# Router logits with the router's columns as loaded weights in the four column quarters of TensorE

## What is computed

```python
shared = geglu(xf, w1s, w2s, w3s)
logits = xf @ Wg                       # (2048 x 256) @ (256 x 8)
idx = jnp.argmax(logits, axis=-1)
for e in range(N_EXPERTS):
    y = geglu(xf, W1[e], W2[e], W3[e])
    final = final + jnp.where((idx == e)[:, None], y, 0.0)
```

## Time and profile before

| | us |
|---|---|
| median of 3 runs | 510.26 |
| lowest, highest | 509.38, 511.22 |
| the profiled execution, its own time | 505.81 |
| its span, first to last instruction | 504.2 |

### The profile page before, as it was taken

How to read it: one execution, slowest core, us unless ns; L and a number is a source line. 1 busy time by engine, 2 the same in 40 slices (tenths; PEclk the granted TensorE clock), 3 DMA queues, 4 the chain that set the end, 5 groups by cost and what they waited for, 6 DMA issues and landing times.

```text
span 504.2 us, 9444 instructions
## 1 busy us (share of the span) xinstructions
PE 492.4 (98%) x2928; PEld 433.9 (86%) x2929; DVE 320.6 (64%) x529; ACT 248.9 (49%) x378; POOL 75.1 (15%) x97
## 2 busy tenths in 40 slices
PE   8999999999999999999999899999999999999994
PEld 7799888888888889898888788988988988988884
DVE  2577768768767778667544876734775568375335
ACT  3676774565653563424444574534572556272220
POOL 4421031011011001004340100100100001000570
PEclk9999999999999999999999999999999999999999
DMA  4997010000000004001342545620745175300235
GB/s 128 359 319 229 2 42 1 0 1 2 1 1 1 1 0 168 2 0 49 129 168 94 207 174 195 237 75 21 239 151 192 41 271 176 127 27 15 73 96 177
DMA packets 20586, 52.81 MB, mean 105 GB/s; under 512 B 3280, under 2 KB 14544, under 8 KB 16592
## 3 DMA queue, kind: packets, MB, share of 16 engines
q0 software_dynamic: 5328, 28.32, 16.0%
q1 hardware_dynamic: 15232, 24.15, 14.0%
HBM read 41.71 MB, written 10.75 MB: 104 GB/s over the span
## 4 chain that ended last, share of the span: by engine, by line
PE 84%; issue 4%; DVE 4%; DMA 3%; POOL 2%; ACT 1%; POOLq 0%; DVEq 0%; SPq 0%
PE ps L246 26%; PE ps L248 25%; PE ps L247 25%; PE ps L686 3%; POOL fetched L429 2%; PE ps L589 1%; DMA first_stage<-tok_w_in 1%; PE ps L604 1%; PE ps L531 1%; DMA q<-codebook_in,idx_sb 1%; PE ps L566 1%; PE ps L578 1%; DVE stats L1021 1%; DMA fetched<-y_sorted,pos 1%; DVE fetched L1327 1%
## 5 line engine op out<-in xcount | busy, mean ns | idle before, releaser
L956 DVE TENSOR_TENSOR hT<-ps,hT 128x512 fp32r<-128x512 f32 x64 | 43.9, 686 | 38.7 <-ACT hT L761 21.4
L246 PE MATMUL ps<-w_slots,xTp 128*128 (+1 forms) x160 | 64.2, 401 | 1.6 <-issue 1.5
L248 PE MATMUL ps<-w_slots,xTp 128*128 (+1 forms) x160 | 62.5, 391 | 0.0
L1289 DVE TENSOR_TENSOR w_slots<-stage,w_slots 128x2048 f32 x24 | 54.9, 2291 | 11.9 <-ACT w_slots L896 11.4
L247 PE MATMUL ps<-w_slots,xTp 128*128 (+1 forms) x160 | 62.2, 389 | 0.0
L772 ACT ACTIVATE hT<-ps 128x512 fp32r<-128x512 f32 x32 | 19.2, 599 | 56.1 <-DVE ps L962 56.1
L246 PE MATMUL ps<-w_slots,gTp 128*128 (+1 forms) x160 | 46.8, 293 | 0.0
L248 PE MATMUL ps<-w_slots,gTp 128*128 (+1 forms) x160 | 45.3, 283 | 0.0
L247 PE MATMUL ps<-w_slots,gTp 128*128 (+1 forms) x160 | 45.2, 283 | 0.0
L1270 DVE TENSOR_TENSOR g_buf<-ps,gelu_buf 128x512 f32<-128x512 f32 x40 | 26.8, 686 | 28.2 <-PE ps L248 28.2
L962 DVE TENSOR_TENSOR ps<-ps,gelub 128x512 f32<-128x512 f32 x32 | 22.3, 698 | 33.8 <-PE ps L248 33.6
(11 more groups left out here) (183 smaller groups left out, 1278.6 us busy)
## 6 DMA issues: line engine op xcount, KB each, us to landing
stage<-ew_in POOLq DMA_DIRECT2D x18, 1024.0 KB, 5.1
stage<-ew_in SPq DMA_DIRECT2D x6, 1024.0 KB, 5.0
x_sorted<-zero_row SPq DMA_DIRECT2D x23, 128.0 KB
x_row<-x_sorted SPq DMA_DIRECT2D x21, 128.0 KB, 2.0
y_sorted<-y_row SPq DMA_DIRECT2D x20, 128.0 KB, 1.7
out_rows<-fetched SPq DMA_DIRECT2D x3, 512.0 KB, 3.0
first_stage<-tok_w_in SPq DMA_DIRECT2D x1, 1024.0 KB, 5.0
first_stage<-tok_w_in SPq DMA_DIRECT2D x2, 512.0 KB, 5.6
```

The source lines that it names most:

```text
L246: pe.matmul(dst, lhs_hi, rhs_hi, start=start, stop=False, skip_group_check=shares_bank)
L248: return pe.matmul(dst, lhs_lo, rhs_hi, start=False, stop=stop, skip_group_check=shares_bank)
L956: dve.tensor_tensor(hT[:, c % RING, 1, :], ps[:, bank, :], f32(hT[:, c % RING, 0, :]), ALU.subtract).then_inc(h_lo, 1)
L1289: dve.tensor_tensor(w_slots[:, bass.ds(to + (PART + c * WCH), WCH)], stage[:, c, :], f32(w_slots[:, bass.ds(to + c * WCH, WCH)]), ALU.subt ...
```

## The change

The logits of a block are computed with the operands swapped. `wgs` is widened from 8 to 32 columns, of which the last 24 are zero (a new memset on DVE at the start, and a load of wgs into the first 8 of 32 columns). Its 128x32 piece is loaded as weights into one quarter of the array's columns, and 128 columns of `xlT` move through it. Row tile i uses quarter i, so the block's logits come out transposed: 32 partitions for each row tile, 128 columns. That takes 8 fp32 matmuls as before. Then DVE copies the 128x128 result to SBUF (`copy_logits`), PE transposes it (`turn_logits`), and DVE takes the 8 used columns of each 32 (`take_logits`). Two semaphores are added, `logits_copied` and `turned_ps`.

```diff
-    LOG = {43: 3}
-    LOG_END = {31: 0, 38: 1, 41: 2}
+    LOG = {31: 0, 41: 2, 43: 3}
+    LOG_END = {38: 1}
+    TURN = {39: 1}
+    TURN_END = {31: 0, 41: 2, 43: 3}
...
-                for i in range(BT):
-                    for k in range(KD):
-                        last = pe.matmul(ps[:, FLIP, i * EXPERTS:(i + 1) * EXPERTS], xlT[:, k, i * P:(i + 1) * P],
-                                         wgs[:, k, :], start=(k == 0), stop=(k == KD - 1))
+                for k in range(KD):
+                    for i in range(BT):
+                        rows = slice(i * QUARTER, (i + 1) * QUARTER)
+                        last = pe.matmul(ps[rows, FLIP, 0:P], wgs[:, k, :], xlT[:, k, i * P:(i + 1) * P], start=(k == 0),
+                                         stop=(k == KD - 1), tile_position=(0, i * QUARTER))
                 last.then_inc(logit_ps, 1)
+
+            def turn_logits(b):
+                pe.wait_ge(logits_copied, b + 1)
+                pe.transpose(ps[:, FLIP, 0:P], logits_turned[:], ident[:]).then_inc(turned_ps, 1)
...
+            def copy_logits(b):
+                dve.wait_ge(logit_ps, b + 1)
+                dve.tensor_copy(logits_turned[:], ps[:, FLIP, 0:P]).then_inc(logits_copied, 1)
+
             def take_logits(b):
-                dve.wait_ge(logit_ps, b + 1)
-                dve.tensor_copy(logits[:, b * BT:(b + 1) * BT, :].rearrange("p t e -> p (t e)"),
-                                ps[:, FLIP, 0:BT * EXPERTS]).then_inc(logits_taken, 1)
+                dve.wait_ge(turned_ps, b + 1)
+                dve.tensor_copy(logits[:, b * BT:(b + 1) * BT, :],
+                                ps[:, FLIP, 0:P].rearrange("p (t e) -> p t e", e=QUARTER)[:, :, 0:EXPERTS]).then_inc(logits_taken, 1)
```

More of the change, by code:

```diff
@@ L168, in build @@
         shift_by = small("shift_by", [P, 1])
-        wgs = small("wgs", [P, KD, EXPERTS])
+        QUARTER = P // 4
+        wgs = small("wgs", [P, KD, QUARTER])
+        logits_turned = small("logits_turned", [P, P])
         stats = small("stats", [P, BT, 6])
@@ L231, in build @@
         x2_ps = sem("x2_ps"); xb_hi = sem("xb_hi"); xb_lo = sem("xb_lo"); xl_act = sem("xl_act");
-        logit_ps = sem("logit_ps"); logits_taken = sem("logits_taken"); onehot_steps = sem("onehot_steps"); onehot_done = sem("onehot_done")
+        logit_ps = sem("logit_ps"); logits_copied = sem("logits_copied"); turned_ps = sem("turned_ps"); logits_taken = sem("logits_taken"); onehot_steps = sem("onehot_steps"); onehot_done = sem("onehot_done")
         rank_ps = sem("rank_ps"); router = sem("router"); placed = sem("placed"); routed = sem("routed"); scattered = sem("scattered")
@@ L280, in _ @@
             sp.dma_start(bh[:], gru_bh).then_inc(small_land, 16)
-            sp.dma_start(wgs[:], wg).then_inc(small_land, 16)
+            sp.dma_start(wgs[:, :, 0:EXPERTS], wg).then_inc(small_land, 16)
             w2v = tok_w2.rearrange("p k n -> p (k n)")
@@ L639, in _ @@
                     q_transposes(QT[c])
-                if c == RANK:
-                    rank_products()
                 if c == ROW:
@@ L644, in _ @@
                     row_transposes(0)
+                if c in TURN:
+                    turn_logits(TURN[c])
                 if c in UNIT:
@@ L658, in _ @@
                     router_logits(LOG_END[c])
+                if c in TURN_END:
+                    turn_logits(TURN_END[c])
+                if c == RANK:
+                    rank_products()
             def up_half(i, slot, n):
@@ L939, in _ @@
             dve.memset(ones[:], 1.0)
+            dve.memset(wgs[:, :, EXPERTS:QUARTER], 0.0)
             dve.memset(half[:], 0.5)
@@ L1184, in _ @@
                     state_rows(3)
-                if c - 1 in LOG_END:
-                    take_logits(LOG_END[c - 1])
+                if c - 1 in TURN_END:
+                    take_logits(TURN_END[c - 1])
+                if c == RANK:
+                    choose_experts()
                 if c % HC == LAG + 1 and HC < c < MLP + HC:
@@ L1195, in _ @@
                     shared_gated(c)
+                    if c in LOG:
+                        copy_logits(LOG[c])
+                    if c in TURN:
+                        take_logits(TURN[c])
                     if c == 32:
@@ L1210, in _ @@
                         normalise(2, 3)
+                elif c in LOG:
+                    copy_logits(LOG[c])
                 chunk_lo(c)
@@ L1226, in _ @@
                     x1_split_lo(X1T[c])
-                if c in LOG:
-                    take_logits(LOG[c])
                 if c in H0:
@@ L1243, in _ @@
                     row_moments(2, 0)
+                if c in LOG_END:
+                    copy_logits(LOG_END[c])
                 if c == 38:
@@ L1254, in _ @@
                     split_piece_lo(n)
-                if c == 43:
-                    choose_experts()
                 if c == RANK:
```

## The result

The changed kernel took 508.48 us (median of 9 runs, 507.75 to 509.9) against 510.99 us for the kernel before (9 runs), timed beside it. The ratio that all runs give is 0.9963, with an interval of 0.9945 to 0.998: 1.9 us faster, between 1.0 and 2.8 (the two medians alone differ by 2.5). Forecast were 509.2 us, a gain of 1.1, and a range of 507.4 to 511.8. So the time lies in the range, 0.7 us under the forecast. The traces say that the gain up to the end of the routed tiles is about twice what was forecast, and that the step in which the quarters of the array overlap was sized wrong.

The account below looks back on a forecast made before the run. PE was taken as the bound from the logits through the routed tiles. A block was to cost 1.33 us against 1.78; 3 x 0.45 - 0.25 = 1.1 saved, 510.26 - 1.1 = 509.2 us, range 507.4 to 511.8.

Parts of the forecast that it names:

- The bound: PE bounds from the logits to the end of the routed tiles, so time saved there moves the whole remainder forward.
- The price of the old logits: Old logits on PE: 1.70 us for 16 records plus 0.08 behind them, 1.78 a block, paced by 128-column weight loads.
- The products in quarters: New logit matmuls on PE: eight start 0.11 us apart, the last has one record more, 0.99 a block; chance 0.50.
- The rival of the entire overlap: All four quarters run side by side: products 0.44 us a block, 2.8 saved, 507.5 us; chance 0.14.
- In and out: Entering and leaving the quartered array on PE: 0.08 us each way, between nothing and 0.16.
- The rival of exposed loads: Loads wait for the product in flight: 0.14 us a record, 2.7 a block, 513.9 us in all; chance 0.06.
- The turn: PE's transpose of the copied logits: 0.10 us plus 0.08 behind it, 0.18 a block.
- The wait of 0.2 feared for block 0: With entirely parallel quarters PE would reach block 0's turn at 138.95 and wait 0.2 us for DVE's copy.
- Block 1: PE waits 0.7 us before the state transposes for DVE's take; the place comes 0.25 late, however fast the quarters.
- Blocks 2 and 3: Low part of x just in time in block 2, rank result waits for DVE in block 3; 0.45 us saved each.
- The sum: Three blocks save 0.45 us each, block 1 loses 0.25: 1.1 us saved, 509.2 us.
- The start: The memset and narrower `wgs` load pieces in the first microseconds, where nobody waits for them: costed at nothing.

Follow-up runs that it names:

- Before_again: The kernel before, unchanged, profiled and timed a second time on one chip with the changed kernel: profiled execution 509.15 us, median 509.62.
- probe: Changed kernel plus a second group of 8 logit matmuls ahead of each block's own: one quarter 1.77 us, two 0.9, four 0.46, four with same-quarter neighbours (block 1) 0.46.
- The three experiments on DVE's order: Changed kernel, block 1: turned logits taken before gating (0.9938 of before); copy before last unit's values, take before statistics (0.9949); besides, statistics behind gating (0.9932).
- the best of them: Changed kernel, but in block 1 DVE copies logits ahead of the last unit's values and takes them ahead of the statistics: 506.76 us, 0.9949 of before.
- turn_at_once: Changed kernel, but PE turns the logits of blocks 0, 2 and 3 directly behind them, ahead of the down product: 1.0012 of before.

## Why the prediction was right, and where it was not

The time fell into the range, and the way the gain comes about was forecast: PE is the bound, the waits in block 1 eat that block's gain, the other turns are covered. The sum behind the 509.2 was wrong in three terms of a block: the products in quarters 0.53 us too dear, the ways in and out 0.15 too cheap, the turn 0.07 too dear. Together they halved the gain. That the time still lay within the range is owed to its width, which took in a rival with a chance of 0.14, and to a whole effect that is small against the range; it is no merit of the sum.

**The bound.** Right. A gain of 2.3 us on PE around the logits reached the last routed tile as 2.2 to 2.5.

**The price of the old logits**, 1.78 us a block: right. Before_again has the same 1.70 us and the same longer pitch behind them, and the gain in the places fits it. That the load of 128 columns paces a record is a reading: in the trace of before the block's 16 load records, 0.19 us each, stand in one group from 188.74 to 190.72, but the probe's group on one quarter has the same pitch of 0.11 with loads of 32 columns, so no run separates the load from the rest of a record.

**The products in quarters: the term that was mis-sized.** It said 9 x 0.11 = 0.99, since the two records of a matmul go to the same quarter and only neighbours in different quarters run side by side. Measured were 0.46: that is the time from one group of 16 to the next in the probe's blocks 1 and 3, four pitches of 0.11 and 0.02 more behind the first four. The premise of the step was that a matmul starts only when both records of the one before it have; that was the author's assumption, which no row of before showed. The runs showed otherwise: in block 0 of the probe three records of line 619 start at 138.18, ahead of the last of line 595 at 138.28, although PE's list has them behind it, so what is said at the start, that each engine works through its list in order, does not hold for these records. The rival of the entire overlap, given 0.14, is what happened; its 2.8 us were not reached because it took the way in as free and the way out at 0.08.

**In and out: mis-sized the other way.** 0.08 each way was taken, between nothing and 0.16. The way in shows as a pitch of 0.32 in place of 0.23: 0.09, so that half was right. The way out was not: where an ordinary product follows the group, in after and in the probe's second groups, it starts 0.55 to 0.58 behind the group's start, not 0.46, and the pitch behind it is longer by 0.10 to 0.11, where the old products made it 0.08 longer. The way out costs some 0.22 in all, in and out 0.31 against the 0.16 of the sum. The sum of both agrees with the prediction's high bound of 2 x 0.16 = 0.32, but it lies mostly on the way out. In the rows of after, both ways the next product starts 0.07 before the last record ends, where it starts 0.16 before between like products.

**The loads.** The rival of exposed loads, given 0.06, put a record at 0.14. With all records on one quarter the probe has 0.11, so nothing comes on top for the loads. The quarter of 0.106 for a load of 32 columns was an estimate: in after the load records of line 597 last 0.106 to 0.110, where those of line 589 in before, 128 columns each, last 0.187 to 0.193.

**The turn.** 0.18 was forecast. A single transpose between down and up product holds PE for 0.04 (138.67 to 138.71) and the pitch behind it is 0.07 longer: 0.11. The 0.10 of a transpose in a row of eight was no measure for one alone. (Behind the wait of block 1 it is 0.17: 191.52 to 191.60, and 0.08 behind it.)

```profile
138.55 0.28 PE L254 MATMUL ps<-w2p,hT 128*128 128x256 f32 x1
138.67 0.27 PE L603 MATMUL ps<-ident,logits_turned 128*128 128x128 f32 x1
138.71 0.47 PE L252 MATMUL ps<-xb_first,w_slots 128*128 128x512 f32 x1
139.01 0.39 PE L253 MATMUL ps<-xb_first,w_slots 128*128 128x512 f32 x1
```

So a block costs 0.09 + 0.46 + 0.22 + 0.11 = 0.88, not 1.33, and saves 0.90, not 0.45. In blocks 0, 2 and 3 the places show 0.8 to 0.9. The wait of 0.2 feared for block 0 did not come: DVE's copy ended at 138.55, and the turn started at 138.67, one usual pitch behind the down product.

```profile
138.27 0.28 DVE L1113 COPY logits_turned<-ps 128x128 f32<-128x128 f32 x1
```

**Block 1.** Right in mechanism and size. Forecast were a loss of 0.25 at the state transposes whatever the quarters do, and a wait of about 0.7 ahead of them. From the logits to the state transposes it was 6.00 us before and 6.30 now (counted from where the logits could have started): 0.30 lost, with waits of 0.23 and 0.60. Of the forecast's terms in that path the 0.04 for the semaphore had no row: in before PE started 0.05 behind DVE's end once (159.89 to 159.94), and ahead of the state transposes it now took 0.14 (193.73 to 193.87). The shorter products only made the waits longer, and the second wait, ahead of the turn, had not been forecast. The three experiments on DVE's order show that the longer wait is for `take_logits`, and the best of them got 0.85 of it back.

**Blocks 2 and 3.** Right: the low part of x came just in time, and the rank products' result waited for DVE.

**The sum.** With the measured terms 3 x 0.90 - 0.30 = 2.4, measured 2.3 in the trace and 1.9 (1.0 to 2.8), 2.5 and 2.4 in three timings. The forecast's 1.1 is half of it. It lay within the range because the range had been drawn to the parallel case, near its 507.5.

**The start.** Costed at nothing. The first down product came 0.5 earlier in after than in the first execution of before, but before_again had it as early (17.61 against 17.69), so that is no effect of the change.

## What to carry to other kernels

The small fp32 products of this kernel, with 32 columns of weights, could be spread over the four column quarters: the records on the same quarter added up at 0.11 us each for 128 moved columns, the quarters ran side by side with two matmuls in a row on the same one (eight in a row held up the others, the numbers between were not tried), and going in and out cost 0.3 us a group. What decided the gain is the detour that the swapped operands need, here a copy and a transpose: it needed other work for PE between its steps, a down product of 1.44 us, and without it the wait for DVE, 2.6 us in all, took all of the gain back (turn_at_once, 1.0012 of before). Before an edit is blamed or praised for its one profiled execution, compare the same place of the program in both traces, since an unrelated standstill at the end was about twice as large as the whole effect.

## What the runs showed of the hardware that I had not expected

- Records of matmuls for different column quarters started out of the program's order: in block 0 of the probe three of line 619 at 138.18, ahead of the last of line 595 at 138.28. In block 1, 16 records with four in a row on the same quarter started in four groups of four, 0.11 us apart.
- That has an end. The probe fits one waiting matmul for each quarter that later ones may pass: behind eight matmuls on quarter 0 those for the free quarters started 0.01 us behind the start of the eighth, 1.56 us after that of the first.
- Going into the quarters cost 0.09 us in after, and coming out 0.22 with the longer pitch behind it, where the old fp32 products of before had 0.08.
- A single transpose between fp32r products cost PE 0.11 us in block 0 of after: 0.04 to the next start, and 0.07 in the longer pitch behind it.
- On two of the four chips whose number is on record PE slowed to one matmul in 0.7 to 1.65 us for some 5 us near the end of the program, in either kernel, with ACT and DVE idle for most of it (in after from 484 to 490). After's first execution had it too. In four of these seven executions the granted clock fell to 0.5 as well, in three it did not. The medians of before are 4 to 4.5 us longer there. Its cause was not found.
- In one execution the granted clock fell to 0.5 for 3.4 us, 0.9 us behind an idle stretch of 1.4 us on PE at the entry of a loop; an idle stretch of 1.4 to 1.5 us is there in every other execution, without the fall.
